# Window attention on one core: values in 32-column tiles, and the inverse deviation moved from ScalarE to GpSimd

## The reference, cut to what matters

```python
xn = (x - mu) * rsqrt(var + 1e-5) * g + b              # per token, over 96 channels
xs = roll(xn, (-4, -4))                                # 4 windows of 8x8 tokens per image
q, k, v = xw @ qkv_w + qkv_b                           # 12 heads of 8 channels, 64 tokens a window
attn = softmax(q * SCALE @ k.T + bias + mask)          # 64x64 for each head and window
out = (attn @ v) @ proj_w + proj_b
x = shortcut + roll(out, (4, 4))
```

## Time and profile before

| What | Value |
|---|---|
| median of the three runs | 512.71 us |
| the profiled execution | 512.89 us, of which the trace spans 511.1 us |
| PE busy / weight loads busy | 488.5 us / 312.7 us |
| DVE busy | 371.9 us |
| ACT busy | 292.6 us |
| POOL busy | 190.3 us |

### The profile page before, as it was taken

How to read it: one execution, slowest core, us unless ns; L and a number is a source line. 1 busy time by engine, 2 the same in 40 slices (tenths; PEclk the granted TensorE clock), 3 DMA queues, 4 the chain that set the end, 5 groups by cost and what they waited for, 6 DMA issues and landing times. The chain is left out here.

```text
span 511.1 us, 22940 instructions
## 1 busy us (share of the span) xinstructions
PE 488.5 (96%) x8866; PEld 312.7 (61%) x8866; DVE 371.9 (73%) x1016; ACT 292.6 (57%) x740; POOL 190.3 (37%) x222
## 2 busy tenths in 40 slices
PE   7999999999999999999888997889999999999996
PEld 7777777777777777777643332325565556555563
DVE  2599999999999999998775362356776565565543
ACT  2477788777787777886564353143444444444332
POOL 8543444443434434344250413035325332332300
PEclk8899999999999999999999999889999999999998
DMA  4211011111011110100033142356543444434311
GB/s 81 64 35 33 21 26 49 31 31 27 21 31 31 31 31 21 40 1 3 3 74 74 32 99 53 82 130 150 137 128 98 127 110 117 114 103 130 106 38 34
DMA packets 41180, 32.55 MB, mean 64 GB/s; under 512 B 19240, under 2 KB 36776, under 8 KB 41128
## 3 DMA queue, kind: packets, MB, share of 16 engines
q1 hardware_dynamic: 36872, 25.36, 19.4%
q0 software_dynamic: 3584, 5.72, 5.1%
q10 hardware_dynamic: 672, 0.75, 0.5%
HBM read 18.36 MB, written 7.13 MB: 50 GB/s over the span
## 5 line engine op out<-in xcount | busy, mean ns | idle before, releaser
L379 POOL TENSOR_TENSOR scores<-scores,peak 128x768 f32<-128x768 f32 x64 | 94.2, 1472 | 129.8 <-DVE peak L548 129.8
L1033 POOL DMA_DIRECT2D x_stack<-padded_x x96 | 52.2, 547 | 95.8 <-PE ps_hidden L1552 63.6
L442 ACT COPY probs_t<-ps_probs 128x768 f32<-128x768 f32 x64 | 51.1, 798 | 40.4 <-PE ps_probs L702 40.3
L540 DVE TENSOR_TENSOR scores<-ps_scores,bias 128x768 f32<-128x768 f32 x64 | 61.3, 958 | 5.6 <-PE ps_scores L692 3.8
L548 DVE TENSOR_REDUCE peak<-scores 128x12 f32<-128x768 f32 x64 | 61.0, 953 | 2.4
L715 PE MATMUL ps_out<-v_blocks,probs_t 128*64 128x54 f32 x1536 | 57.1, 224 | 1.0 <-ACT out_t L447 0.9
L715 PEld LDWEIGHTS ps_out<-v_blocks,probs_t 128*64 128x64 f32 x1536 | 50.2, 138 | 12.3 <-issue 12.2
L436 ACT ACTIVATE scores<-scores 128x768 f32<-128x768 f32 x64 | 54.2, 847 | 1.5 <-POOL scores L379 1.5
L702 PE MATMUL ps_probs<-ident,scores 128*128 128x128 f32 x384 | 54.3, 277 | 0.0
L1140 ACT ACTIVATE hidden<-ps_hidden,fc_b_folded 128x512 f32<-128x512 f32 x44 | 26.6, 688 | 39.3 <-PE ps_hidden L1469 38.8
L1552 PE MATMUL ps_turn<-x_stack,conv_w 40*32 40x256 f32 x1536 | 48.8, 379 | 0.0
(11 more groups left out here) (159 smaller groups left out, 850.9 us busy)
## 6 DMA issues: line engine op xcount, KB each, us to landing
x_stack<-padded_x POOLq DMA_DIRECT2D x96, 54.0 KB, 2.7
x_stack<-padded_x SPq DMA_DIRECT2D x96, 54.0 KB
padded_x<-x_pad SPq DMA_DIRECT2D x26, 121.5 KB, 2.6
x_sliced<-stream SPq DMA_DIRECT2D x48, 64.0 KB, 2.0
stream<-y_sliced SPq DMA_DIRECT2D x48, 64.0 KB, 2.0
out<-out_sb SPq DMA_DIRECT2D x32, 96.0 KB, 2.2
x_now<-in_x SPq DMA_DIRECT2D x32, 72.0 KB, 1.8
stream<-in_x SPq DMA_DIRECT2D x32, 72.0 KB, 1.9
```

The lines of the kernel that those rows point to most:

```text
L379: nc.gpsimd.tensor_tensor(sc, sc, peak[:, par, p, :].unsqueeze(2).to_broadcast((128, HEADS, WN)), ALU.subtract).then_inc(s["shifted"], 1)
L442: nc.scalar.copy(probs_t[:, :], ps_turned).then_inc(s["turned_copied"], 1)
L540: nc.vector.tensor_tensor(scores[:, par, p, :].rearrange("p (g c) -> p g c", g=NG), ps_scores[:, :, 0:GROUP * WN], bias[:, p, :].rearrange ...
L1033: engine.dma_start(x_stack[64 * half + i * HC:64 * half + (i + 1) * HC, slot, :, :], rows).then_inc(landed[slot], 16)
```

## The change

The inverse deviation is made by two GpSimd instructions (an addition of epsilon, and a power with the exponent -0.5 from a new tile of one column) in the place of ScalarE's two. GpSimd does it for image 0 behind the issue of its 16 DMAs and ahead of the clearing of `v_blocks`, for image 1 between the two halves of `bias`, and for image t+1 at the head of its step t, for t from 1 to 30. The waits stay the same ones; ScalarE's `scale` follows on `rstd_ready` as before.

`make_v` and `weigh` use stationary operands of 32 columns, four to the 128 output partitions: 16 matmuls of 48 streamed columns in the place of 8, and 24 of 18 streamed columns in the place of 12 of 54. `v_blocks` loses its two further groups.

```diff
--- before.py
+++ after.py
@@ -232,7 +232,8 @@
     q_sb = sb("q_sb", [C, N])
     k_blocks = sb("k_blocks", [C, GROUP, N])
 
-    v_blocks = sb("v_blocks", [128, 2, PAIRS, 2, HP + 2, 2, VC])
+    v_blocks = sb("v_blocks", [128, 2, PAIRS, 2, HP, 2, VC])
+    exponent = sb("exponent_window", [128, 1])
     scores = sb("scores", [128, 2, PAIRS, SC])
     peak = sb("peak", [128, 2, PAIRS, HEADS])
     probs_t = sb("probs_t", [128, SC])
@@ -348,6 +349,7 @@
     @block.gpsimd
     def _(pool):
         nc.gpsimd.memset(eps[:, :], EPS).then_inc(zeroed, 1)
+        nc.gpsimd.memset(exponent[:, :], -0.5).then_inc(zeroed, 1)
 
         table = a["L0_conv_rel_bias"]
         for upper in range(2):
@@ -357,12 +359,25 @@
                 at = upper * WN + y * WS
                 pool.dma_start(rel_rows[at:at + WS, :, :].rearrange("p (r c) h -> p r (c h)", r=WS),
                                runs).then_inc(rel_in, 16)
+        def inverse_deviation(t):
+
+            pool.wait_ge(s["spread_ready"], (t + 1) * 2)
+            need(pool, s["rstd_ready"], t)
+            nc.gpsimd.tensor_tensor(log_var[:, :], spread[:, :, 1], eps[:, 0:1].to_broadcast((128, 2)),
+                                    ALU.add).then_inc(s["log_ready"], 1)
+            pool.wait_ge(s["log_ready"], t + 1)
+            need(pool, s["scaled_ready"], t * 2)
+            nc.gpsimd.tensor_tensor(rstd[:, :], log_var[:, :], exponent[:, 0:1].to_broadcast((128, 2)),
+                                    ALU.pow).then_inc(s["rstd_ready"], 1)
+
+        pool.wait_ge(zeroed, 2)
+        inverse_deviation(0)
         nc.gpsimd.memset(v_blocks[:, :, :, :, :, :, :], 0.0).then_inc(zeroed, 1)
-        pool.wait_ge(zeroed, 2)
+        pool.wait_ge(zeroed, 3)
         for e in range(2):
             for par in range(2):
                 nc.gpsimd.memset(v_blocks[64 * e:64 * e + 64, par, :, :, :, e, HD:VC], 1.0).then_inc(zeroed, 1)
-        pool.wait_ge(zeroed, 6)
+        pool.wait_ge(zeroed, 7)
         nc.gpsimd.memset(w_late["final"][:, :], 0.0).then_inc(zeroed_final, 1)
         pool.wait_ge(rel_in, 16 * 2 * WS)
         pool.wait_ge(second_in, 16 * SECOND)
@@ -371,6 +386,8 @@
                                     rel_rows[:, ::-1, :].rearrange("p m h -> p h m"),
                                     shift_mask[:, p, :].unsqueeze(1).to_broadcast((128, HEADS, WN)),
                                     ALU.add).then_inc(bias_set, 1)
+            if p == 0:
+                inverse_deviation(1)
 
         def subtract_peak(t, p, par):
             u = t * 2 + p
@@ -379,7 +396,10 @@
             nc.gpsimd.tensor_tensor(sc, sc, peak[:, par, p, :].unsqueeze(2).to_broadcast((128, HEADS, WN)),
                                     ALU.subtract).then_inc(s["shifted"], 1)
 
+
         def step(t, half, par):
+            if not is_image(t, 0) and not is_image(t, B - 1):
+                inverse_deviation(t + 1)
             subtract_peak(t, 0, par)
             subtract_peak(t, 1, par)
 
@@ -390,15 +410,6 @@
 
     @block.scalar
     def _(act):
-        def inverse_deviation(t):
-
-            act.wait_ge(s["spread_ready"], (t + 1) * 2)
-            need(act, s["rstd_ready"], t)
-            nc.scalar.activation(log_var[:, :], spread[:, :, 1], ACT.Ln, bias=eps[:, 0:1]).then_inc(s["log_ready"], 1)
-            act.wait_ge(s["log_ready"], t + 1)
-            need(act, s["scaled_ready"], t * 2)
-            nc.scalar.activation(rstd[:, :], log_var[:, :], ACT.Exp, scale=-0.5).then_inc(s["rstd_ready"], 1)
-
         def scale(t):
             act.wait_ge(s["rstd_ready"], t + 1)
             need(act, s["turned_back"], t)
@@ -422,7 +433,7 @@
 
         def copy_v(t, par):
             if is_image(t, 0):
-                act.wait_ge(zeroed, 6)
+                act.wait_ge(zeroed, 7)
             act.wait_ge(s["v_ready"], t + 1)
             need(act, s["pv_ready"], (t - 1) * 2)
 
@@ -447,7 +458,6 @@
             nc.scalar.copy(shifted(out_t[:, par, :], p), window_rows(ps_ot, p)).then_inc(s["ot_copied"], 1)
 
         nc.scalar.preload_act_table_set("natural_log_exp_and_others")
-        act.wait_ge(zeroed, 1)
 
         def step(t, half, par):
             if real(t):
@@ -461,7 +471,6 @@
             if real(t + 2):
                 copy_q(t + 2)
             if real(t + 3):
-                inverse_deviation(t + 3)
                 scale(t + 3)
             if real(t + 1):
                 copy_turned(t + 1, 0)
@@ -674,9 +683,10 @@
             need(pe, s["residual_done"], t - 2)
             heads = w_qkv[:, 2 * C:3 * C].rearrange("c (q e d) -> c q e d", e=2, d=HD)
             for window in range(2 * PAIRS):
-                for e in range(2):
-                    mm = nc.tensor.matmul(ps_v[64 * e:64 * e + 64, window, :, :], normed[:, window * WN:(window + 1) * WN],
-                                          heads[:, :, e, :], start=True, stop=True, skip_group_check=True)
+                for quarter in range(4):
+                    at = window * WN + 32 * (quarter % 2)
+                    mm = nc.tensor.matmul(ps_v[32 * quarter:32 * quarter + 32, window, :, :], normed[:, at:at + 32],
+                                          heads[:, :, quarter // 2, :], start=True, stop=True, skip_group_check=True)
             mm.then_inc(s["v_ready"], 1)
 
         def score(t, p):
@@ -711,10 +721,11 @@
             need(pe, s["ot_copied"], u)
             pe.wait_ge(s["turned_copied"], u + 1)
             for q in range(HP):
-                for top in range(2):
-                    mm = nc.tensor.matmul(ps_out[64 * top:64 * top + 64, 0, q * 2 * VC:(q + 3) * 2 * VC],
-                                          probs_t[:, q * 128 + 64 * top:q * 128 + 64 * top + 64],
-                                          v_blocks[:, par, p, top, q:q + 3, :, :].rearrange("p q e c -> p (q e c)"),
+                for quarter in range(4):
+                    rows = slice(32 * quarter, 32 * quarter + 32)
+                    mm = nc.tensor.matmul(ps_out[rows, 0, q * 2 * VC:(q + 1) * 2 * VC],
+                                          probs_t[:, q * 128 + 32 * quarter:q * 128 + 32 * quarter + 32],
+                                          v_blocks[:, par, p, quarter // 2, q, :, :].rearrange("p e c -> p (e c)"),
                                           start=True, stop=True, skip_group_check=True)
             mm.then_inc(s["pv_ready"], 1)
 
```

## The result

The changed kernel took 541.90 us in the median of four runs (540.60 to 543.08), the kernel before 515.92 us beside it; the ratio is 1.054 (95% interval 1.048 to 1.060), so it is slower by 5.4%. (The ratio leaves out one disturbed run of the kernel before that its median holds.) The profiled execution took 542.07 us, its span is 540.3 us, 29.2 more than before.

What follows compares the result with a forecast made beforehand. It took VectorE to bound the loop's step, TensorE close behind. The 512.9 us before, plus 18.3 for the loop (30 x 0.61) and 4.3 for the start, gave 535.5 us, range 515 to 553.

Steps and rivals of the forecast that it cites:

- What bounds the kernel: Attention loop: VectorE sets the 7.02 us step, TensorE close behind; the second bias addition has next to no slack.
- TensorE was the bound: Rival for the loop: it gets faster, by at most 30 x 0.21 = 6 us; chance 0.02.
- ScalarE loses Ln and Exp, worth nothing: Loop on ScalarE: dropping Ln and Exp (0.29 and 0.20 us) gains nothing, as ScalarE is busy 5.70 of 7.05 us.
- GpSimd's price: GpSimd's new addition 0.25 us and power 0.59 us, with the gap 0.94 us per inverse deviation.
- The rivals of a cheap and of a dear power: GpSimd's pair: cheap as a memset, 516.5 us, chance 0.13; power with large fixed part, 563 to 608 us, chance 0.09.
- Where they lie: GpSimd's queue: the pair sits behind the previous image's second subtract_peak, so scale starts 1.47 us later.
- TensorE's tiles: make_v and weigh on TensorE: weigh to score 0.58 us instead of 0.85, make_v to weigh 0.28 instead of 0.46.
- The rival that they start no closer than today: Thin weigh tiles on TensorE: second score waits 1.64 us instead of 0.58, 567 us in all; chance 0.05.
- The loop's chain: From scale through copy_turned, weigh and score: second bias addition 0.61 us later each step, 30 x 0.61 = 18.3 us.
- The start: Image 0's inverse deviation waits for GpSimd's 16 DMA issues, until 10.57 us; whole start 4.3 us later.
- the clock: TensorE's granted clock in the loop: if it falls in the new waits, the step is longer than forecast; no size given.
- the ring: Loop: GpSimd's power delays second score, next find_peak and so next subtract_peak; paid once a step, 0.61 us.

Runs made afterwards that it cites:

- e1_tiles_only: Changed kernel with the inverse deviation back on ScalarE (Ln and Exp), only the 32-column tiles left; 507.64 us, ratio 0.987 to the kernel before.
- e5: Changed kernel with image t+2's inverse deviation between GpSimd's two subtractions and image 0's on ScalarE; 507.91 us, ratio 0.986 to the kernel before.
- e4: Changed kernel with GpSimd's order turned: image t+2's inverse deviation between the two subtractions of image t; 512.24 us, ratio 0.996 to the kernel before.
- e3: Changed kernel with only image 0's inverse deviation back on ScalarE's Ln and Exp; 535.95 us, ratio 1.046 to the kernel before.
- e6_power_twice: Changed kernel with a second, unread GpSimd power of the same size ahead of the real one; 571.89 us, ratio 1.111 to the kernel before.
- e9: e1_tiles_only plus six GpSimd additions and six powers of 1 to 32 elements per partition behind the attention loop; 514.02 us, run once.
- e7: Changed kernel with make_v back at 64 columns, weigh kept at 32; 545.16 us, ratio 1.057 to the kernel before.
- e8: Kernel before with only weigh in tiles of 32 columns, make_v and inverse deviation untouched; 507.25 us, ratio 0.984 to the kernel before.

## Why the prediction was right

It gave 535.5 us and the likeliest mechanism; 541.9 came, by that mechanism, along a path that had one wait more than I had counted. Step by step:

- *What bounds the kernel.* Right that the second addition has no slack, wrong that the step is VectorE's: e1_tiles_only has 6.86 us with VectorE's work untouched. Of the 0.21 us that I allowed as the most that TensorE could give back, 0.16 were there. That is why the tiles alone are worth 1.3%, and the rival "TensorE was the bound" had more to it than its chance of 0.02 says, though its 2% were not reached.
- *ScalarE loses Ln and Exp, worth nothing.* Shown by e5 against e1.
- *GpSimd's price.* 0.19 + 0.69 us with a gap of 0.09 to 0.16 between them, 0.97 to 1.04; I had 0.25 + 0.59 + 0.1 = 0.94. The sum was near by luck, because two errors met: the power's fixed part is 0.42, not an addition's 0.25, and an addition costs less than I took. The rivals of a cheap and of a dear power are both out.
- *Where they lie.* Shown by e4: 0.89 us of a settled step go with the order alone. The sign that I had named, the second addition idle for about 0.6 us, came in two parts: in the step shown VectorE waits 0.44 us for `weigh` ahead of `weigh_heads`, and then the 0.23 us for the score.
- *TensorE's tiles.* `weigh`: 0.58 us from its first load to that of the score, as predicted from the row of the channel attention; its 48 loads take 0.53 us, (0.53 - 0.11) / 47 = 9 ns apart. The rival that they start no closer than today is out. (The floor of about 25 ns in the Trainium skill, TensorE: Matmul & The Clock Gate, Part 1, is not what this trace shows: 48 of them would fill an estimated 1.2 us.) `make_v`: 0.33 in e1 in place of the predicted 0.28; in the changed kernel a copy of ScalarE's is last, as predicted, but not the copy that I had named.
- *The loop's chain.* 0.61 predicted, 0.73 measured in the settled steps. The term that was mis-sized is what `weigh` waits for. I let it start 0.05 us behind the end of `copy_turned`; it starts 0.21 behind it (141.21 to 141.42), 0.16 more. `weigh` also waits on `ot_copied`, that is for the `copy_ot` of the pair before, which reads `ps_out`, the tile that `weigh` writes. I had named `copy_ot` as queued behind `copy_turned` on ScalarE, but had left it off the path. It ends at 141.35, and `weigh` loads 0.07 behind it; so it is, within 0.01, in each of its 20 steps from 48 to 196 us. Two copies that always follow each other can't be told apart in those steps, but the last `weigh` of the attention parts them:

```profile
271.88 0.80 ACT L453 COPY probs_t<-ps_probs 128x768 f32<-128x768 f32 x1 [0.60 <-PE ps_probs L712]
...
272.94 0.27 ACT L458 COPY out_t<-ps_out 96x128 f32<-96x128 f32 x1
...
273.29 0.53 PEld L726 LDWEIGHTS ps_out<-v_blocks,probs_t 128*32 128x32 f32 x48 [1.26 <-issue]
...
273.32 0.60 PE L726 MATMUL ps_out<-v_blocks,probs_t 128*32 128x18 f32 x48 [0.93 <-ACT out_t L458]
```

  There `copy_turned` is over at 272.68 and `copy_ot` at 273.21, and `weigh` loads at 273.29: 0.61 us behind the one, 0.08 behind the other, and the trace puts the wait of its matmuls down to `copy_ot`. About half of the 0.16 was made good by smaller errors: `copy_turned` follows `scale` by 0.47 and not 0.54, `scale` comes 2.51 us behind the end of `find_peak` and not 2.54, and the addition follows the score's loads by 0.85, not 0.83. That gives the 7.70 us of the step shown. Every other step takes about 0.1 more; in those the power stands 0.16 us behind its addition and not 0.09. Over 29 steps the 0.12 are 3.5 us.
- *The start.* 4.3 predicted, 4.9 in the trace, 5.2 by e3's. The power's longer row is a part of it, and TensorE's clock another: from 12 to 14 us it was granted 0.50, the 1.2 GHz level, and `turn_back` lasts 0.66 us, where it took 0.42 before, granted 0.97 from 7 to 8.8 us.
- *Not in the sum: the clock*, named only among what could make it wrong. Stretches of the changed kernel (TensorE busy, granted clock):

```profile
28.00:30.00 2.00, 0.70 (x13) 1.00 0.63 164
30.00:32.00 2.00, 1.35 (x60) 0.75 0.00 0
32.00:34.00 2.00, 2.00 (x53) 0.50 0.04 8
34.00:36.00 2.00, 2.00 (x10) 0.50 0.21 50
```

TensorE waits for 0.9 and 1.0 us around 28 and 30 us, is busy for 0.70 of 2.00, and is then granted 0.50, the 1.2 GHz level, from 32 to 36 us. The two steps there take 8.48 and 8.50 us, 1.5 more than two settled ones. e4, with the same late start but no ring, is granted 1.00 there, and its first two steps take 6.79 and 7.15 us; e3, with the ring but the old start, is granted 0.50 from 26 to 32 us, and its first two take 8.72 and 8.36. The dip comes with the ring.

Put together, in us: 0.6 at the start, 3.5 in the chain, 1.5 of the clock, and 1.8 behind the attention that other kernels vary by as well, less 0.6 since the loop was counted as 30 steps and its growth lies in 29: 6.8, within 0.2 of the 6.6 that 29.2 is over the predicted 22.6.

What stays open: why the power stands 0.16 us behind its addition in every other step and 0.09 in the rest, and why the clock falls in some steps of e6_power_twice and not in the next. No run takes these apart.

## What to carry to other kernels

An instruction moved onto an idle engine is paid by its place in that engine's queue, not by the engine's idle share: here GpSimd had 4 of 7 us free, and the same two instructions cost 0.89 us a step behind one neighbour and nothing ahead of it. Before such a move, follow the ring: from the end of what stands ahead of it in the queue through all that waits for its result, and see whether it comes round to the same instruction an image later. At each link, count every wait that the code names, not only the one whose data is needed: here the wait left out was for a copy out of the tile that `weigh` writes, and it came 0.16 us behind what I had counted, in every step. And split a change that has two parts by experiment even where the sum was foreseen: here one part was worth 1.3%, hidden under the other's loss.

## What the runs showed of the hardware that I had not expected

- GpSimd's power has a fixed part of some 0.42 us beside 0.156 us for each element of a partition (e9), where an addition has 0.19 and next to nothing.
- A change of tile shape between neighbours costs TensorE: thin `weigh` starts 0.60 to 0.61 us behind the first load of wide `make_v` (e7, e8), against 0.46 where both are wide and 0.33 where both are thin (e1). Where both have one shape, the loads of `weigh` begin 0.08 to 0.09 us before those of `make_v` are over; where the shape changes, 0.05 behind their end. The Trainium skill, TensorEngine Tiling (Array Packing), Key Properties, says that changing the tiling mode drains the engine; the trace agrees, with 0.14 to 0.15 us as the difference to the wide pair.
- The granted clock can alternate from step to step: in e6, from 183 to 218 us, steps granted 0.81 and 1.00 follow each other, and the same work takes 9.03 to 9.07 or 8.46 to 8.47 us.
